# Order of a turn: two projection pieces directly behind the scores, then the transposes of both heads in one run

## The chip, the core and the metric

The kernel runs on one core of a Trainium2 chip. The core has several engines that run side by side, each through its own queue, in order: TensorE (PE in the rows; its weight loads are PEld), VectorE (DVE), ScalarE (ACT), GpSimd (POOL) and SyncE (SP, which issues DMAs here). They wait for each other only at semaphores. The metric is the device time of one execution in microseconds (us).

## The reference

Two layers over an input x of 8 sequences x 512 tokens x 256 channels. What the change touches is the attention of the first layer, with 16 heads of 64:

```python
q = _rmsnorm(q, q_rms_w); k = _rmsnorm(k, k_rms_w)      # after the projections x @ Wq, x @ Wk, x @ Wv
gate = softplus(einsum('bthd,hd->bht', k, u_n) / sqrt(D))
bias = -dist * omega_eff * gate                         # -inf above the diagonal
attn = softmax(q k^T * scale + bias)
y = attn @ v;  x = x + y @ Wproj + expert part
```

Beside it stand a first-layer expert part (32 experts, routed ahead of the attention, whose feed-forward is spread over the attention) and a second layer (memory read and routed feed-forward), which follows as a stage of its own.

## The kernel before, in words

The program has three stages: routing, attention (`attend`), second layer. Attention is a loop over 64 turns `s`: a turn is one sequence and one pair of heads (8 pairs per sequence). Each engine has its own loop over the same turns with its steps written out by hand; that text is the order. Nothing schedules it otherwise.

A turn is software-pipelined. In turn `s` TensorE does, in this order before the change:

- `all_scores(s)` (L939): scores of both heads into PSUM banks, in four causal chunks of 512, 256, 384 and 128 columns. It needs q and k of turn `s`, in a high and a low part (`qT_hi`, `kT_hi` from ScalarE; `qT_lo`, `kT_lo` from VectorE).
- `turn_p0(s-1)` (L978): 10 transposes of the probabilities of head 0 of the turn before, into three banks (4, 3 and 3 transposes).
- `project(s+2, 0)` and `project(s+2, 1)` (L926): 6 matmuls each; the projection of q, k, v and gate input for the turn after next, one 128-token piece each.
- `turn_p1(s-1)` (L978): 10 transposes for head 1.
- in some turns `turn_hidden` (L1025), then `project(s+2, 2)`.
- `values(s-1)` (L1006): probabilities times v. It waits for all six copies of transposed probabilities (`probT`): four by ScalarE (L1201), two by VectorE (L1371, one per head, the bank with the fifth to seventh transpose).
- the expert's matmuls (L1017 or L1034), the transposes of q, k and the gate columns for turn `s+1` (`turn_q` L959, `turn_k` L964, `turn_aug` L970), and `project(s+2, 3)`.
- in every eighth turn the output projection (L1050).

VectorE in a turn: `lows` (L1348, row minimum of the scores, 8 instructions in four pairs), and between them `mean_square(s+1)` (L1297 and L1300, sums of squares of q and k); `take_raw` (L1293, projection piece 0 from PSUM); `copy_p(s-1, 0)` (L1371); `newton_step` (L1304 to L1308, the inverse root, which waits for ScalarE's estimate); `copy_p(s-1, 1)` (L1371); then `copy_hidden` in some turns (L1388), gate input (L1316, L1318), `norm` (L1326), `gate` (L1322), `divide` (L1355, L1361), the expert's bias or output (L1383 or L1393), `copy_y` (L1377), `low_q` (L1333), `low_k` (L1338) and the second half of `divide`.

ScalarE in a turn: `square` (L1156), `exps(s,3)` and `exps(s,1)` (L1192), `copy_p` of head 0 (L1201 twice), `rsqrt(s+1)` (L1160, L1163: the estimate from the sums of squares), `take_raw` (L1149, piece 1), `copy_p` of head 1 (L1201 twice), further exponentials, `gate` (L1168, L1170), `copy_y` (L1206), `copy_q` (L1175), `copy_k` (L1179), `copy_aug` (L1183). In every fourth turn (`s % 4 == 2`, called gelu turn below) it puts `gelu` (L1210, with two table loads) ahead of the copies, and the exponentials behind them.

GpSimd's `augment` (L1479 to L1491) makes the gate columns `ag` from `gate`'s result; `turn_aug` on TensorE waits for them.

So four kinds of turn alternate, told apart by `s % 4`: 0 and 1 begin an expert (L1017), 2 is the gelu turn, 2 and 3 end an expert (L1025, L1034).

Of the kernel before, what the change touches and what calls it, by code (L numbers as in the profile page):

```python
# [674 lines left out]
def attend(nc, t, out, g):  # L675
# [5 lines left out]
    NTURN = B * HP  # L681
# [11 lines left out]
    with ExitStack() as ctx:  # L693
# [86 lines left out]
        def begins_in(s):  # L780

            return 2 * (s // 4) + s % 4 if s < NTURN and s % 4 < 2 else None

        def ends_in(s):

            return 2 * (s // 4) + s % 4 - 2 if s < NTURN and s % 4 >= 2 else None
# [44 lines left out]
        with nc.Block() as block:  # L831
# [80 lines left out]
            def _(eng):  # L912
# [70 lines left out]
                def turn_p0(s):  # L983
                    eng.wait_ge(p_done.sem, p_done.at(s, 1))
                    for i in range(3):
                        if s + 1 < NTURN:
                            eng.wait_ge(maxed.sem, maxed.at(s + 1, i + 1))
                        turn_p(s, 0, i)

                def turn_p1(s):  # L990
                    eng.wait_ge(p_done.sem, p_done.at(s, 2))
                    for i in range(3):
                        if s + 1 < NTURN:
                            eng.wait_ge(maxed.sem, maxed.at(s + 1, (4, 7, 8)[i]))
                        turn_p(s, 1, i)
# [103 lines left out]
                for s in range(NTURN + 1):  # L1099
                    if s < NTURN:  # L1100
                        all_scores(s)
                    else:
                        eng.wait_ge(y_done.sem, y_done.at(s - 2))
                        eng.wait_ge(eo_done.sem, eo_done.at(E - 1))
                    if s > 0:
                        turn_p0(s - 1)
                    if s + 2 < NTURN:
                        eng.wait_ge(o_done.sem, o_done.at((s - 1) // HP - 1))
                        project(s + 2, 0)
                    prepare(s, 0)  # L1110
                    if s + 2 < NTURN:
                        project(s + 2, 1)
                    prepare(s, 1)
                    if s > 0:
                        turn_p1(s - 1)
                    if ends_in(s) is not None:
                        turn_hidden(ends_in(s), s)
                    if s + 2 < NTURN:
                        project(s + 2, 2)
                    prepare(s, 2)  # L1120
                    if s > 0:
                        values(s - 1)
                    if begins_in(s) is not None:
                        hidden(begins_in(s), s)
                    if ends_in(s) is not None:
                        expert_output(ends_in(s), s)
                    if s + 1 < NTURN:
                        if s == 0:
                            eng.wait_ge(maxed.sem, maxed.at(0, 8))
                        turn_q(s + 1)  # L1130
                        turn_k(s + 1)
                        turn_aug(s + 1)
                    if s + 2 < NTURN:
                        project(s + 2, 3)
                    prepare(s, 3)
                    if 0 < s < NTURN and s % HP == 0:
                        for n in range(NT):
                            output(s // HP - 1, n)
# [3 lines left out]
            def _(eng):  # L1142
# [15 lines left out]
                def rsqrt(j):  # L1158
                    eng.wait_ge(ssd.sem, ssd.at(j))
                    eng.activation(lnv[:, :], ss[:, :], ACT.Ln).then_inc(r0_done.sem, 1)  # L1160
                    eng.wait_ge(newton.sem, newton.at(j - 1))
                    eng.wait_ge(r0_done.sem, r0_done.at(j, 1))
                    eng.activation(r0[:, :], lnv[:, :], ACT.Exp, scale=-0.5).then_inc(r0_done.sem, 1)  # L1163
# [31 lines left out]
                def copy_p(s, h, i):  # L1195
                    pe_p, done = (pe_p0, pe_p1)[h], (pt0_A, pt1_A)[h]
                    if h == 0 and i == 0:
                        eng.wait_ge(pe_y.sem, pe_y.at(s - 1))
                    eng.wait_ge(pe_p.sem, pe_p.at(s, i + 1))
                    x, y = segT[i]  # L1200
                    eng.activation(probT[h][:, x:y], bP[h][i][:, 0:y - x], ACT.Copy).then_inc(done.sem, 1)  # L1201
# [37 lines left out]
                for s in range(NTURN + 1):  # L1239
                    if s + 1 < NTURN:  # L1240
                        square(s + 1)
                    if s % 4 == 2:
                        gelu(s // 4)
                    elif s < NTURN:
                        exps(s, 3)
                        exps(s, 1)
                    if s > 0:
                        copy_p(s - 1, 0, 0)
                        copy_p(s - 1, 0, 2)
                    prepare(s, 0)  # L1250
                    if s + 1 < NTURN:
                        rsqrt(s + 1)
                    if s + 2 < NTURN:
                        take_raw(s + 2, 1)
                    prepare(s, 1)
                    if s > 0:
                        copy_p(s - 1, 1, 0)
                        copy_p(s - 1, 1, 2)
                    if s % 4 == 2:
                        exps(s, 3)  # L1260
                        gate(s + 1)
                        exps(s, 1)
                    if s < NTURN:
                        exps(s, 2)
                    if s + 1 < NTURN and s % 4 != 2:
                        gate(s + 1)
                    if s + 2 < NTURN:
                        take_raw(s + 2, 2)
                    prepare(s, 2)
                    if s < NTURN:  # L1270
                        exps(s, 0)
                    if s > 0:
                        copy_y(s - 1)
                    if s in (1, 2):
                        part = slice((s - 1) * HP // 2, s * HP // 2)
                        eng.wait_ge(wp_load.sem, wp_load.at(0))
                        eng.activation(wp_hi[:, part, :], proj_in[:, part, :], ACT.Copy).then_inc(wp_hi_done.sem, 1)
                    if s + 1 < NTURN:
                        copy_q(s + 1)
                        copy_k(s + 1)  # L1280
                        copy_aug(s + 1)
                    if s + 2 < NTURN:
                        take_raw(s + 2, 3)
                    prepare(s, 3)
# [3 lines left out]
            def _(eng):  # L1288
# [139 lines left out]
                for s in range(NTURN + 1):  # L1428
                    if s < NTURN:
                        lows(s, 3)  # L1430
                        lows(s, 1)
                    if s + 1 < NTURN:
                        mean_square(s + 1)
                    if s < NTURN:
                        lows(s, 2)
                        lows(s, 0)
                    if s + 2 < NTURN:
                        take_raw(s + 2)
                    prepare(s, 0)
                    if s > 0:  # L1440
                        copy_p(s - 1, 0)
                    prepare(s, 1)
                    if s + 1 < NTURN:
                        newton_step(s + 1)
                    if s > 0:
                        copy_p(s - 1, 1)
                    if ends_in(s) is not None:
                        copy_hidden(ends_in(s))
                    if s + 1 < NTURN:
                        gate_input(s + 1)  # L1450
                        norm(s + 1)
                        gate(s + 1)
                    if s < NTURN:
                        divide(s, 0)
                    if begins_in(s) is not None:
                        add_bias(begins_in(s))
                    prepare(s, 2)
                    if ends_in(s) is not None:
                        copy_expert_output(ends_in(s))
                    if s > 0:  # L1460
                        copy_y(s - 1)
                    if s + 1 < NTURN:
                        low_q(s + 1)
                        low_k(s + 1)
                    if s < NTURN:
                        divide(s, 1)
                    prepare(s, 3)
                    if 0 < s < NTURN and s % HP == 0:
                        for n in range(NT):
                            output(s // HP - 1, n)  # L1470
# [500 lines left out]
```

## Time and profile before

| what | value |
|---|---|
| executions, median of 3 | 1359.23 us (1357.82 to 1359.45) |
| profiled execution, span from the first to the last instruction | 1353.4 us |
| profiled execution's own time | not listed apart; the median is 5.8 us over the span |
| PE busy, share of the span | 97% |
| DVE busy | 81% |
| ACT busy | 70% |
| POOL busy | 14% |
| attention stage in the span | about 87 to 1085 us |

A matmul's row reads longer than the step from one to the next, since matmuls overlap in the array; the start times tell the pace. In a row, "xN" merges N like instructions, and "[0.23 <-PE at L926]" is idle time of the engine before the row and what ended it.

### The profile page before, as it was taken

How to read it: one execution, taken by the hardware profiler on the slowest of the kernel's cores; microseconds unless marked ns; L12 is line 12 of the kernel's file. 1: busy time of each engine (PE TensorE's matmuls, PEld its weight loads, DVE VectorE, ACT ScalarE, POOL GpSimd, SP SyncE). 2: the span in 40 equal slices, each digit the busy share in tenths (PEclk: the TensorE clock that was granted, in tenths of full speed). 3: DMA queues.
4: the chain of work that ended last, by engine and by line, in shares of the span. 5: the costliest groups of instructions: out<-in, count | busy, mean ns of one | idle time of the engine just before them, and what ended most of it. 6: DMA issues, size and time to landing. Idle time of an engine off the chain costs nothing. (4 is left out here: it accounts for less than half of the span.)

```text
span 1353.4 us, 32125 instructions
## 1 busy us (share of the span) xinstructions
PE 1309.2 (97%) x11499; PEld 1103.9 (82%) x11499; DVE 1090.3 (81%) x3337; ACT 947.7 (70%) x2376; POOL 190.3 (14%) x564
## 2 busy tenths in 40 slices
PE   5899999999999999999999999999999799999999
PEld 3688888887978888797888878888888588888888
DVE  6869996999699789969996998799699867777663
ACT  6759885888588678858885887688598724444333
POOL 4512111111011111101111111111111100000000
PEclk8889999999999999999999999999999999999999
DMA  6452231332323222322322233233232322111100
GB/s 216 171 173 88 73 132 59 110 116 74 102 74 131 80 89 87 104 88 88 119 93 92 84 102 109 67 108 103 77 99 72 108 82 62 55 56 55 55 17 32
DMA packets 90831, 125.17 MB, mean 92 GB/s; under 512 B 8761, under 2 KB 77105, under 8 KB 90673
## 3 DMA queue, kind: packets, MB, share of 16 engines
q1 hardware_dynamic: 90352, 123.11, 28.2%
q8 instruction: 93, 1.52, 0.5%
q14 instruction: 66, 0.53, 0.1%
q10 hardware_dynamic: 320, 0.00, 0.0%
HBM read 103.69 MB, written 19.40 MB: 91 GB/s over the span
## 5 line engine op out<-in xcount | busy, mean ns | idle before, releaser
L1192 ACT ACTIVATE prob<-prob,low 128x512 f32<-128x512 f32 (+3 forms) x512 | 280.8, 551 | 115.7 <-DVE low L1348 115.7
L1348 DVE CUSTOM_DVE_ANT_0 prob<-at,mask 128x512 f32<-128x512 f32 (+3 forms) x512 | 219.6, 485 | 10.3 <-PE at L939 10.3
L926 PE MATMUL at<-w_hi,c_lo 128*128 128x386 f32 x512 | 190.1, 371 | 1.5 <-DVE area_raw L1293 1.5
L926 PE MATMUL at<-w_hi,c_hi 128*128 128x386 f32 x512 | 174.3, 340 | 0.0
L926 PE MATMUL at<-w_lo,c_hi 128*128 128x386 f32 x512 | 174.0, 340 | 0.0
L1361 DVE TENSOR_SCALAR prob<-prob,rec 128x512 f32<-128x512 f32 (+3 forms) x512 | 169.3, 394 | 4.5
L978 PE MATMUL at<-ident,prob 128*128 128x128 f32 x1280 | 164.3, 275 | 3.2 <-DVE low L1348 1.8
L1006 PE MATMUL at<-probT,v 128*32 128x512 f32 (+3 forms) x2048 | 152.6, 438 | 3.8 <-DVE probT L1371 2.6
L978 PEld LDWEIGHTS at<-ident,prob 128*128 128x128 f32 x1280 | 142.4, 140 | 10.6 <-DVE yT_lo L1377 1.6
L1006 PEld LDWEIGHTS at<-probT,v 128*32 128x32 f32 x2048 | 67.3, 110 | 89.8 <-issue 80.7
L1201 ACT ACTIVATE probT<-at 128x512 f32<-128x512 f32 (+1 forms) x256 | 130.3, 536 | 4.4 <-PE at L978 1.5
L1479 POOL TENSOR_TENSOR slope<-gl,omega 128x8 f32<-128x8 f32 x64 | 12.8, 200 | 842.8 <-DVE gl L1322 821.9
L1149 ACT ACTIVATE area_raw<-at 128x386 f32<-128x386 f32 x192 | 93.4, 486 | 21.6 <-PE at L926 19.5
L926 PEld LDWEIGHTS at<-w_hi,c_lo 128*128 128x128 f32 x512 | 97.3, 190 | 2.2 <-DVE area_raw L1293 1.8
L926 PEld LDWEIGHTS at<-w_lo,c_hi 128*128 128x128 f32 x512 | 97.6, 191 | 0.1
L926 PEld LDWEIGHTS at<-w_hi,c_hi 128*128 128x128 f32 x512 | 96.8, 189 | 0.0
L1192 ACT ACTIVATION_READ_ACCUMULATOR prob<-prob,low 128x1 f32 x512 | 96.7, 189 | 0.0
L939 PE MATMUL at<-kT_hi,qT_hi 64*128 64x512 f32 (+3 forms) x512 | 86.6, 331 | 6.6 <-ACT kT_hi L1179 6.6
L939 PE MATMUL at<-kT_lo,qT_hi 64*128 64x512 f32 (+3 forms) x512 | 85.1, 326 | 1.5
L939 PE MATMUL at<-kT_hi,qT_lo 64*128 64x512 f32 (+3 forms) x512 | 84.7, 324 | 0.0
L939 PE MATMUL at<-kaug,qaug 64*128 64x512 f32 (+3 forms) x512 | 83.6, 319 | 0.0
L1297 DVE TENSOR_REDUCE ssq<-area_sq 128x16 f32<-128x1024 f32 x64 | 77.7, 1214 | 1.6 <-ACT area_sq L1156 1.6
(254 smaller groups left out, 3195.9 us busy)
## 6 DMA issues: line engine op xcount, KB each, us to landing
area_w<-in_L_ffn_w SPq DMA_DIRECT2D x65, 1024.0 KB, 5.5
bias<-in_L_ffn_w SPq DMA_DIRECT2D x160, 32.0 KB, 4.4
x_in<-in_L_attn_x SPq DMA_DIRECT2D x8, 512.0 KB, 5.5
xr<-in_L_attn_x SPq DMA_DIRECT2D x8, 512.0 KB, 4.6
eo_d<-hidT SPq DMA_DIRECT2D x32, 128.0 KB, 1.8
x_d<-xr SPq DMA_DIRECT2D x8, 512.0 KB, 2.9
area_raw<-x_d SPq DMA_DIRECT2D x8, 512.0 KB, 3.9
out<-area_raw SPq DMA_DIRECT2D x7, 512.0 KB, 3.1
```

What stands on the lines that cost most here:

```text
L926: m = eng.matmul(bQ[n % 2][:, 0:W], a[:, (j // HP) % 2, k, n * P:(n + 1) * P], w[:, k, j % HP, :], start=start, stop=(k == KC - 1 and a is ...
L939: m = eng.matmul(bC[i][:, at:at + (c + 1) * P], q[rows, c * P:(c + 1) * P], k[rows, 0:(c + 1) * P], start=ready is k_hi_done, stop=q is qaug)
L978: m = eng.transpose(bP[h][i][:, at:at + P], prob[s % 2][h][:, off[c] + kc * P:off[c] + (kc + 1) * P], ident[:, :])
L1006: m = eng.matmul(bY[rows, kc * P:T], v[:, s % 2, kc, rows], probT[j * E // D][:, offT[kc]:offT[kc + 1]], start=(kc == 0), stop=(kc == NT - 1))
L1149: eng.activation(raw[:, j % 2, n, :], bQ[n % 2][:, 0:W], ACT.Copy).then_inc(raw_A.sem, 1)
L1192: eng.activation(sl, sl, ACT.Exp, scale=-1.0, bias=low[:, i:i + 1], accum_out=den[:, i:i + 1]).then_inc(exp_done.sem, 1)
L1201: eng.activation(probT[h][:, x:y], bP[h][i][:, 0:y - x], ACT.Copy).then_inc(done.sem, 1)
L1297: eng.tensor_reduce(ss[:, :], sq[:, :, :].rearrange("p n (i d) -> p (n i) d", d=D), AX.X, ALU.add).then_inc(ssd.sem, 1)
L1348: eng.tensor_tensor_reduce(out=prob[s % 2][h][:, off[c]:off[c + 1]], in0=bC[i][:, at:at + (c + 1) * P], in1=mask[:, (NT - 1 - c) * P:T], s ...
L1361: p = eng.tensor_scalar(sl, sl, rec[:, k:k + 1], None, ALU.mult)
L1479: eng.tensor_tensor(slope32[:, :, :], gl[:, :, :], omega[:, hp * 2:hp * 2 + 2].unsqueeze(1).to_broadcast([P, NT, 2]), ALU.mult).then_inc(a ...
```

## The change

It changes only the order of steps in three of the engines' loops; no instruction is added or removed.

- TensorE: `turn_p0(s-1)` moves from directly behind the scores to behind `project(s+2, 1)`, directly ahead of `turn_p1(s-1)`.
- VectorE: `mean_square(s+1)` moves from between the `lows` to behind `copy_p(s-1, 0)`; `copy_p(s-1, 1)` comes ahead of `newton_step(s+1)`; `prepare(s, 1)` (used in the last turns only) comes ahead of both copies.
- ScalarE: all four `copy_p` stand together behind `take_raw(s+2, 1)`, and `rsqrt(s+1)` behind them.

```diff
@@ TensorE
-                    if s > 0:
-                        turn_p0(s - 1)
                     if s + 2 < NTURN:
                         eng.wait_ge(o_done.sem, o_done.at((s - 1) // HP - 1))
                         project(s + 2, 0)
...
                     prepare(s, 1)
                     if s > 0:
+                        turn_p0(s - 1)
                         turn_p1(s - 1)
@@ ScalarE
-                    if s > 0:
-                        copy_p(s - 1, 0, 0)
-                        copy_p(s - 1, 0, 2)
                     prepare(s, 0)
-                    if s + 1 < NTURN:
-                        rsqrt(s + 1)
                     if s + 2 < NTURN:
                         take_raw(s + 2, 1)
                     prepare(s, 1)
                     if s > 0:
+                        copy_p(s - 1, 0, 0)
+                        copy_p(s - 1, 0, 2)
                         copy_p(s - 1, 1, 0)
                         copy_p(s - 1, 1, 2)
+                    if s + 1 < NTURN:
+                        rsqrt(s + 1)
@@ VectorE
                         lows(s, 3)
                         lows(s, 1)
-                    if s + 1 < NTURN:
-                        mean_square(s + 1)
-                    if s < NTURN:
                         lows(s, 2)
                         lows(s, 0)
                     if s + 2 < NTURN:
                         take_raw(s + 2)
                     prepare(s, 0)
+                    prepare(s, 1)
                     if s > 0:
                         copy_p(s - 1, 0)
-                    prepare(s, 1)
+                    if s + 1 < NTURN:
+                        mean_square(s + 1)
+                    if s > 0:
+                        copy_p(s - 1, 1)
                     if s + 1 < NTURN:
                         newton_step(s + 1)
-                    if s > 0:
-                        copy_p(s - 1, 1)
```

VectorE's queue in a turn that ends an expert, before, from the last pair of `lows` on (the four rows of the 384- and 128-column `lows` have `mean_square` ahead of them):

```order
L1297 TENSOR_REDUCE ssq<-area_sq 128x16
L1300 TENSOR_SCALAR ssq<-ssq 128x16
L1348 ISA prob,low<-at,mask 128x384
...
L1293 COPY area_raw<-at 128x386
L1371 COPY probT<-at 128x384
L1304 SCALAR_TENSOR_TENSOR nw<-r 128x16
L1306 TENSOR_TENSOR nw<-nw,ssq 128x16
L1308 SCALAR_TENSOR_TENSOR rs<-nw,r 128x16
L1371 COPY probT<-at 128x384
L1388 COPY hidT<-at 128x256
```

And now (line numbers are two lower):

```order
L1291 COPY area_raw<-at 128x386
L1369 COPY probT<-at 128x384
L1295 TENSOR_REDUCE ssq<-area_sq 128x16
L1298 TENSOR_SCALAR ssq<-ssq 128x16
L1369 COPY probT<-at 128x384
L1302 SCALAR_TENSOR_TENSOR nw<-r 128x16
L1304 TENSOR_TENSOR nw<-nw,ssq 128x16
L1306 SCALAR_TENSOR_TENSOR rs<-nw,r 128x16
L1386 COPY hidT<-at 128x256
```

The sums of squares have moved from ahead of the last `lows` to between the two copies of `probT`, and the inverse root behind both.

ScalarE's queue in a gelu-free turn, from the exponentials to the next ones, before:

```order
L1192 ACTIVATE prob,dens<-prob,low 128x256 x2
L1201 ACTIVATE probT<-at 128x512
L1201 ACTIVATE probT<-at 128x384
L1160 ACTIVATE lnv<-ssq 128x16
L1163 ACTIVATE r<-lnv 128x16
L1149 ACTIVATE area_raw<-at 128x386
L1201 ACTIVATE probT<-at 128x512
L1201 ACTIVATE probT<-at 128x384
L1192 ACTIVATE prob,dens<-prob,low 128x384 x2
```

And now:

```order
L1191 ACTIVATE prob,dens<-prob,low 128x256 x2
L1148 ACTIVATE area_raw<-at 128x386
L1200 ACTIVATE probT<-at 128x512
L1200 ACTIVATE probT<-at 128x384
L1200 ACTIVATE probT<-at 128x512
L1200 ACTIVATE probT<-at 128x384
L1159 ACTIVATE lnv<-ssq 128x16
L1162 ACTIVATE r<-lnv 128x16
L1191 ACTIVATE prob,dens<-prob,low 128x384 x2
```

The logarithm and exponential of the sums of squares (`lnv`, `r`) now stand directly ahead of the next exponentials and behind all four copies.

TensorE's queue behind the scores shows one `L978 MATMUL at<-ident,prob 128x128 x20` behind the twelve L926 matmuls, where a run of ten stood ahead of them and a run of ten behind.

## Rows read from the trace of the kernel before

**Rows 1.** Table by stretch, turns 0, 2, 3 of four: PE, PEld, DVE, ACT, POOL, PEclk, DMA.
```profile
519.75:533.79 14.04, 14.04 (x137) 11.68 (x137) 12.98 (x43) 11.66 (x32) 2.24 (x8) 1.00 0.31 96
...
547.77:562.26 14.49, 14.18 (x139) 11.61 (x139) 13.07 (x43) 14.17 (x35) 2.10 (x7) 1.00 0.40 145
562.26:576.86 14.60, 14.50 (x138) 11.59 (x138) 13.85 (x45) 11.88 (x33) 2.24 (x8) 1.00 0.27 85
```

**Rows 2.** Timeline (start us, length us, ...) of TensorE, turn with `s % 4 == 0`.
```profile
522.27 0.27 PE L939 MATMUL at<-kaug,qaug 64*128 64x128 f32 x2
522.48 1.31 PE L978 MATMUL at<-ident,prob 128*128 128x128 f32 x10
...
525.62 0.34 PE L926 MATMUL at<-w_hi,c_hi 128*128 128x386 f32 x1
525.79 1.25 PE L978 MATMUL at<-ident,prob 128*128 128x128 f32 x10
526.80 0.42 PE L926 MATMUL at<-w_hi,c_lo 128*128 128x386 f32 x1
...
527.76 0.33 PE L926 MATMUL at<-w_hi,c_hi 128*128 128x386 f32 x1
528.09 2.36 PE L1006 MATMUL at<-probT,v 128*32 128x512 f32 x32
```

**Rows 3.** Timeline of TensorE, first turn, which has no transposes of probabilities.
```profile
89.57 0.44 PE L926 MATMUL at<-w_hi,c_lo 128*128 128x386 f32 x1
...
91.62 0.33 PE L926 MATMUL at<-w_hi,c_hi 128*128 128x386 f32 x1
```

**Rows 4.** Timeline of VectorE, the turn of rows 2.
```profile
523.13 1.22 DVE L1297 TENSOR_REDUCE ssq<-area_sq 128x16 f32<-128x1024 f32 x1
...
524.47 0.55 DVE L1348 CUSTOM_DVE_ANT_0 prob<-at,mask 128x384 f32<-128x384 f32 x1
...
526.32 0.55 DVE L1371 COPY probT<-at 128x384 f32<-128x384 f32 x1
526.78 0.16 DVE L1304 SCALAR_TENSOR_TENSOR nw<-r 128x16 f32<-128x16 f32 x1
...
527.28 0.55 DVE L1371 COPY probT<-at 128x384 f32<-128x384 f32 x1
...
531.42 0.42 DVE L1383 TENSOR_TENSOR hid<-at,bias 128x256 f32<-128x256 f32 x1 [0.58 <-issue]
...
532.71 0.75 DVE L1333 SCALAR_TENSOR_TENSOR qT_lo<-at,q_scale,qT_hi 128x512 fp32r<-128x512 f32 x1 [0.27 <-ACT qT_hi L1175]
```

**Rows 5.** Timeline of ScalarE, gelu turn (`s % 4 == 2`).
```profile
553.59 0.22 ACT L1160 ACTIVATE lnv<-ssq 128x16 f32<-128x16 f32 x1
...
555.41 0.71 ACT L1192 ACTIVATE prob<-prob,low 128x512 f32<-128x512 f32 x1
```

**Rows 6.** Timeline of TensorE: first transposes of gelu turn and next, scores between.
```profile
550.46 1.31 PE L978 MATMUL at<-ident,prob 128*128 128x128 f32 x10
...
562.26 0.50 PE L939 MATMUL at<-kT_hi,qT_hi 64*128 64x512 f32 x2 [0.31 <-ACT kT_hi L1179]
...
565.43 1.31 PE L978 MATMUL at<-ident,prob 128*128 128x128 f32 x10
```

**Rows 7.** Timelines of VectorE, GpSimd and weight loads, turn with `s % 4 == 3`.
```profile
570.37 0.55 DVE L1371 COPY probT<-at 128x384 f32<-128x384 f32 x1
...
572.58 0.16 DVE L1322 SCALAR_TENSOR_TENSOR gl<-gl,gp 128x8 f32<-128x8 f32 x1
...
574.40 0.21 POOL L1491 TENSOR_TENSOR ag<-shift,ag 128x8 fp32r<-128x8 f32 x1
...
575.17 0.44 PEld L970 LDWEIGHTS at<-ident,ag 128*68 128x68 f32 x4
```

**Rows 8.** Table by stretch, last turns of the attention (columns as in rows 1).
```profile
1069.00:1076.00 7.00, 4.46 (x34) 3.62 (x34) 5.64 (x21) 6.02 (x17) 0.00 (x0) 1.00 0.52 166
1076.00:1080.00 4.00, 3.61 (x32) 1.39 (x36) 2.56 (x8) 1.60 (x7) 0.00 (x0) 0.57 0.00 0
```

## The prediction

> **What bounds the kernel now.** I read the table by stretch first [rows 1]. A turn takes 14.0 us when `s % 4` is 0 or 1 (one of the two stands there), 14.5 us in the gelu turn and 14.6 us in the turn behind it; 64 turns make up some 1,000 us of the 1353.4 us span. TensorE shows busy for the whole of the first kind (14.04 of 14.04), at the full clock, so that kind looks bound by TensorE. VectorE is busy for 12.98 of 14.04 us, and for 13.85 of 14.60 in the last kind; ScalarE for 14.17 of 14.49 us in the gelu turn. Three engines are close to the length of a turn, so a new wait on VectorE or ScalarE has little room to be made good.
>
> Then the timelines show who is late. In the ordinary turn TensorE's last matmul of `project(s+2,2)` starts at 527.76, and `values` at 528.09 [rows 2]. The step from one such matmul to the next is 0.17 us (525.62 to 525.79), so `values` comes 0.16 us behind that. VectorE's second copy of `probT` starts at 527.28, takes 0.55 and ends at 527.83 [rows 4], 0.26 us ahead of `values`. I take it that this copy is what `values` waits for, and that 0.26 us is the way from its end to the matmul. So TensorE is full up to this point only because VectorE's copy is just in time. That is what I look at most.
>
> In the gelu turn the scores of the next turn wait for ScalarE's `kT_hi` with 0.31 us of idle time [rows 6]: there ScalarE sets the end, without a pause from the gelu on (14.17 us busy).
>
> **The change, part by part.** No instruction is added, so every cost is a wait or a switch.
>
> *TensorE alone.* Before: from the first transpose at 522.48 to the first matmul of `project(s+2,2)` at 526.80 are 4.32 us [rows 2]. After: I take the same gap behind the scores as now (0.21 us, 522.27 to 522.48) [rows 2]; the first turn has the two projection pieces there already, and its twelve matmuls take 89.57 to 91.62 plus 0.17, that is 2.22 us [rows 3]; two runs of ten transposes take 1.01 us each (525.79 to 526.80). Sum 4.24, a gain of 0.08 us a turn: one switch between transposes and matmuls less. Over 61 full turns that is 5 us, if nothing else is late.
>
> *VectorE's two copies, in each turn.* The copy of head 0 needs the seventh transpose of its head. That used to be done long before VectorE came. Now the transposes start at 522.48 + 2.22 = 524.70; the seventh starts six steps of 0.101 later, 525.31, takes the 0.275 us that the last of ten shows (1.25 less nine steps, rounded down) and ends at 525.58. I add 0.06 us for the signal and get 525.64 for the copy, where it was 526.32. VectorE is free 1.34 us earlier than before (`mean_square` left the place ahead: 523.13 to 524.47), at 524.98, and so idles for 0.66 us. Behind the copy (0.46 us to the next start, 526.32 to 526.78) comes `mean_square`, 1.34 us, and only then the copy of head 1: 525.64 + 0.46 + 1.34 = 527.44, against 527.28 [rows 4]. So `values` goes from 528.09 to 528.25: 0.16 us later, where TensorE alone would be 0.08 + 0.08 earlier. The inverse root (0.50 us, 526.78 to 527.28) has left the place ahead of the copy, but the idle time of 0.66 us is more than that.
>
> Everything on TensorE behind `values` is in order and shifts by the same 0.16 us, and the scores of the next turn with it. For 31 turns of the kinds 0 and 1: 31 x 0.16 = 5.0 us. In the kind 3 the first transposes are at 565.43 [rows 6]; by the same working the first copy starts at 565.43 + 2.22 + 0.88 + 0.06 = 568.59 and the second at 570.39, where it was 570.37 [rows 7], so nothing is lost or won at `values`. The bounds for this term: 0 when the signal comes at once and the copies run 0.1 us closer, 0.3 us a turn when each of two signals costs 0.1 us more.
>
> *The inverse root behind both copies.* The sums of squares are done about 1.42 us after `mean_square` starts (1.34 and the tail of its second instruction). ScalarE begins its logarithm 0.09 us later, and that and the exponential, 0.22 us each with a step between [rows 5], are done 0.57 us later, when `newton_step` may start; ScalarE's next instruction, whose start overlaps a little, follows 0.47 us behind the logarithm's start. In the ordinary turn: 526.10 + 1.42 + 0.09 + 0.57 = 528.18, plus 0.50 us for itself: gate input starts at 528.68, where it was 527.74. `norm`, `gate` and `divide` are 0.94 us later. What hides it: VectorE idles 0.58 us before `hid` and 0.27 us before `qT_lo` [rows 4], together 0.85, and these shift by 0.16 with TensorE: 1.01 against 0.94. Costs nothing, but the cover is used up.
>
> *GpSimd's gate columns.* In the kind 3, `gate` on VectorE starts at 572.58, the last of `ag` ends at 574.61 and TensorE's weights for `turn_aug` load at 575.17 [rows 7]: 0.56 us of slack. `gate` is later by 0.79 us (newton done at 568.59 + 0.46 + 1.42 + 0.09 + 0.57 + 0.50 = 571.63, where the queue was free at 570.37 + 0.47 = 570.84, one copy behind its start). So `ag` is done at 575.40, plus 0.08 for the signal: `turn_aug` is 0.3 us late, TensorE with it. 15 x 0.3 = 4.5 us. Bounds: 0 to 0.6 us a turn (GpSimd's spans are rough). In the kinds 0 and 1 the slack is as long as the delay, in the gelu turn the wait lies under ScalarE's.
>
> *ScalarE in the gelu turn.* This is the largest term. Transposes start at 550.46 + 2.22 = 552.68 [rows 6], VectorE's first copy at 552.68 + 0.88 + 0.06 = 553.62, `mean_square` at 554.08, its result at 555.50, logarithm 555.59, and the exponentials of the scores at 555.59 + 0.47 = 556.06, where they were at 555.41 [rows 5]: 0.64 us later. Before, `rsqrt` found its input ready; now it is behind four copies which wait for transposes, and then waits for the sums itself. From there ScalarE has no pause up to `copy_k`, on which the next scores wait. So all 0.64 us are on the path: 15 x 0.64 = 9.6 us. Bounds: 0.4 (TensorE's run and VectorE's copy 0.1 us earlier each) and 0.85. In the other kinds the same delay ends in ScalarE's idle time before `qT_hi`.
>
> *Last three turns.* They have few or no projections; `prepare` takes their place. VectorE and TensorE wait for each other for 1 us and more there, and I cost the edits at nothing, within 1 us either way.
>
> Sum: 5.0 + 4.5 + 9.6 = 19.1 us. Against the profiled execution: 1353.4 to 1372.5 us of span, 5.8 us around it, 1378.3 us. The median of the runs is 5.8 us over the profiled span, so I add 19.1 to 1359.2: 1378 us. The low bounds of the terms give 0 + 0 + 6 = 6 us (1365), the high ones 9.3 + 9 + 12.8 = 31 us (1390).
>
> **A rule against it: the clock.** TensorE had the full clock in all three turns of rows 1. In the last turns it had 1.00 from 1069 to 1076 us, while it was busy for 4.46 of 7.00 us, and 0.57 from 1076 to 1080 us [rows 8], a stretch at the lower of its two levels, 1.2 GHz against 2.4, behind transposes with waits between. Twenty transposes in one run make 2.0 us of such work. The Trainium skill, "TensorE: Matmul & The Clock Gate", Part 4: PE-mode transpose, says that transposes don't count as busy for the clock in the way matmuls do; by that rule a longer run would invite a fall. In rows 1 ten at a time, and twelve of another kind, do not.
>
> **The rivals.**
> *A. Faster.* VectorE's first copy is not held. All three costs hang on its start at 525.64. If it starts when its queue is free, at 524.98, the second copy is 0.5 us earlier than now, the sums come early enough for ScalarE and GpSimd, and `values` follows at TensorE's own pace: 0.16 us a turn in 31 turns and 0.08 in 30, 7 us, that is 1352. It decides below a start of about 525.2, where the gelu term is down to 0.2 us a turn. Against it: the seventh transpose behind twelve matmuls can't be done by then at the paces of rows 2 and 3. For it: TensorE shows as busy without a gap, so its rows may hide slack.
> *B. No difference.* The gain of TensorE and a delay of 0.2 us in gelu turns cancel: 1359, within 0.2%. For it: all other idle time is left. Against it: ScalarE's chain in the gelu turn has none.
> *C. The clock falls in each turn.* At half speed for some 3.4 us the 2.36 us of `values` would stretch by about 1.5 us (half of 3.4 us' work is left, with the waits taken off); over 61 turns some 90 us, 1450. Rows 8 show such a fall only with TensorE idle for a third of the time before it.
> *D. Only the gelu term is real*, and `values` and `ag` are in time: +6 to +10 us, inside my range.
>
> **How the numbers follow.** Forecast with its three terms 0.77, D 0.10, B 0.04, A 0.06, C 0.03. A measurement of this kernel tells 0.2% (2.7 us) from no change. Faster holds A: 0.06, and 0.01 for what I have not seen; same B with a part of D: 0.05; the rest, 0.88, is slower. The time is the forecast's, 1378. The range, 1364 to 1390, takes in the bounds of the terms and D; A, B and C are left out.
>
> **What would show it.** The page's row of `values` on TensorE (L1006) and of the copy of `probT` (L1369 then) with waits between them: VectorE idle about 0.6 us ahead of the first copy in each turn, ended by L978; `values` ending a wait for the copy. TensorE's twelve projection matmuls 0.21 us behind the scores. In the gelu turn, ScalarE's exponentials 0.6 us later against the scores' start, and the turn 15.1 us instead of 14.5. `turn_aug` idle 0.3 us in the turn behind it, ended by GpSimd. An ordinary turn of 14.2 us. The prediction is wrong if the ordinary turn is at or under 14.0 us (the first copy was not late), or if the gelu turn keeps its 14.5 us.

## The result, and the profile after

The changed kernel is slower. The first comparison gave 1374.46 us (median of 4, 1374.04 to 1377.49) against 1358.53 us for the kernel before, a ratio of 1.0157 with a 95% interval of 1.0122 to 1.0192. A second one, with more executions of both side by side, gave 1382.51 us against 1355.73 us, a ratio of 1.0213 (1.0182 to 1.0244). The forecast was 1378 us, within 1364 to 1390. The span of the profiled execution grew from 1353.4 to 1375.8 us.

The medians of one kernel move by some us from comparison to comparison. The stage ahead of the attention is the place: in the traces below, attention begins between 81.2 and 89.0 us, with one and the same code ahead of it, while the stretch behind it takes some 263 us in all twelve. So I compare ratios, and beside them the length of the attention stage alone (from the first scores to the last matmul group of `values`; before, that is from 86.9 to 1090.4 us), which is free of that: 1003.5 us before, 1026.9 us in the changed kernel, 1027.1 us in the second trace of it. The change costs 23.4 us there, a little more than the 19.1 us of the forecast.

The table by stretch of the changed kernel, one row for each kind of turn, `s % 4` of 0 to 3 (us, then busy us of PE, PEld, DVE, ACT and POOL, the granted clock, DMA share and GB/s), answers to [rows 1]:

```profile
529.63:543.86 14.23, 13.98 (x137) 11.65 (x136) 13.02 (x43) 11.96 (x32) 2.24 (x8) 1.00 0.32 94
543.86:558.07 14.21, 13.98 (x138) 11.62 (x138) 13.15 (x43) 11.96 (x32) 2.11 (x7) 1.00 0.26 87
558.07:573.23 15.16, 14.34 (x139) 11.86 (x139) 12.90 (x43) 14.53 (x35) 2.09 (x7) 1.00 0.40 142
573.23:588.11 14.88, 14.78 (x138) 11.82 (x138) 14.00 (x45) 12.22 (x33) 2.25 (x8) 1.00 0.24 80
```

The ordinary turn (`s % 4` of 0 or 1) grew by 0.19 us (the second one by 0.23, from 13.98), the gelu turn by 0.67, the turn behind it by 0.28. These are single turns; over all 31 ordinary ones the growth is 0.27 us a turn. The granted clock is 1.00 in all four rows. TensorE is no longer busy for the whole of an ordinary turn.

TensorE's timeline in the first of these turns answers to [rows 2]; the twelve projection matmuls stand ahead of the run of twenty now:

```profile
534.56 2.34 PE L978 MATMUL at<-ident,prob 128*128 128x128 f32 x20
536.66 0.42 PE L926 MATMUL at<-w_hi,c_lo 128*128 128x386 f32 x1
...
538.20 2.36 PE L1006 MATMUL at<-probT,v 128*32 128x512 f32 x32 [0.25 <-DVE probT L1369]
```

Counted from the scores' start (529.63), `values` begins at 8.57 us, where it was 8.34 (528.09 less 519.75), and now its row itself says what it waited for: VectorE's copy of `probT`. VectorE's timeline of the same turn answers to [rows 4]:

```profile
534.28 0.56 DVE L1291 COPY area_raw<-at 128x386 f32<-128x386 f32 x1
535.59 0.56 DVE L1369 COPY probT<-at 128x384 f32<-128x384 f32 x1 [0.75 <-PE at L978]
536.06 1.21 DVE L1295 TENSOR_REDUCE ssq<-area_sq 128x16 f32<-128x1024 f32 x1
...
537.39 0.55 DVE L1369 COPY probT<-at 128x384 f32<-128x384 f32 x1
538.07 0.18 DVE L1302 SCALAR_TENSOR_TENSOR nw<-r 128x16 f32<-128x16 f32 x1
...
541.73 0.41 DVE L1381 TENSOR_TENSOR hid<-at,bias 128x256 f32<-128x256 f32 x1
...
542.83 0.75 DVE L1331 SCALAR_TENSOR_TENSOR qT_lo<-at,q_scale,qT_hi 128x512 fp32r<-128x512 f32 x1
```

The first copy is held by the transposes for 0.75 us, the sums of squares queue behind it, the second copy behind them. The idle times before `hid` (0.58 us) and `qT_lo` (0.27 us) of [rows 4] are gone: no more cover. ScalarE in the gelu turn answers to [rows 5]:

```profile
563.69 2.18 ACT L1200 ACTIVATE probT<-at 128x512 f32<-128x512 f32 x4
565.95 0.22 ACT L1159 ACTIVATE lnv<-ssq 128x16 f32<-128x16 f32 x1
...
566.38 0.71 ACT L1191 ACTIVATE prob<-prob,low 128x512 f32<-128x512 f32 x1
```

The exponentials start 8.31 us behind the scores' start (558.07), where it was 7.64 (555.41 less 547.77). TensorE's next scores pay for it, in a row that answers to [rows 6]:

```profile
573.23 0.50 PE L939 MATMUL at<-kT_hi,qT_hi 64*128 64x512 f32 x2 [0.81 <-ACT kT_hi L1178]
```

The idle time rose from 0.31 to 0.81 us. In the turn behind, GpSimd's last `ag` row and the weights of `turn_aug` answer to [rows 7]:

```profile
586.24 0.21 POOL L1488 TENSOR_TENSOR ag<-shift,ag 128x8 fp32r<-128x8 f32 x1
...
586.51 0.36 PEld L970 LDWEIGHTS at<-ident,ag 128*68 128x68 f32 x4 [0.22 <-POOL ag L1488]
```

### The profile page after: what moved, and what is told of

The parts are those of the page before. It is cut to its first block and busy times, and to the rows that moved or that the text cites. A ratio compares the mean times of both kernels' runs of the same rounds, so it can differ in the third digit from the quotient of the medians.

```text
span 1375.8 us, 32125 instructions
## 1 busy us (share of the span) xinstructions
PE 1314.2 (96%) x11499; PEld 1107.9 (81%) x11499; DVE 1095.4 (80%) x3337; ACT 967.2 (70%) x2376; POOL 190.0 (14%) x564
## 5 line engine op out<-in xcount | busy, mean ns | idle before, releaser
L1346 DVE CUSTOM_DVE_ANT_0 prob<-at,mask 128x512 f32<-128x512 f32 (+3 forms) x512 | 215.3, 485 | 10.6 <-PE at L939 10.6
L926 PE MATMUL at<-w_hi,c_lo 128*128 128x386 f32 x512 | 191.3, 374 | 0.2 <-DVE area_raw L1291 0.2
L926 PE MATMUL at<-w_hi,c_hi 128*128 128x386 f32 x512 | 174.0, 340 | 0.0
L926 PE MATMUL at<-w_lo,c_hi 128*128 128x386 f32 x512 | 173.6, 339 | 0.0
L1359 DVE TENSOR_SCALAR prob<-prob,rec 128x512 f32<-128x512 f32 (+3 forms) x512 | 165.1, 386 | 4.5
L1006 PE MATMUL at<-probT,v 128*32 128x512 f32 (+3 forms) x2048 | 154.1, 441 | 10.5 <-DVE probT L1369 10.2
L978 PE MATMUL at<-ident,prob 128*128 128x128 f32 x1280 | 150.6, 273 | 1.9 <-DVE prob L1359 1.4
L1006 PEld LDWEIGHTS at<-probT,v 128*32 128x32 f32 x2048 | 72.3, 110 | 95.2 <-issue 87.4
L978 PEld LDWEIGHTS at<-ident,prob 128*128 128x128 f32 x1280 | 143.4, 140 | 5.0 <-DVE yT_lo L1375 1.6
L1200 ACT ACTIVATE probT<-at 128x512 f32<-128x512 f32 (+1 forms) x256 | 135.0, 545 | 5.5 <-PE at L978 1.8
L1476 POOL TENSOR_TENSOR slope<-gl,omega 128x8 f32<-128x8 f32 x64 | 12.8, 200 | 866.5 <-DVE gl L1320 846.3
L1369 DVE COPY probT<-at 128x384 f32<-128x384 f32 x128 | 70.7, 553 | 40.3 <-PE at L978 40.1
L926 PEld LDWEIGHTS at<-w_hi,c_lo 128*128 128x128 f32 x512 | 97.0, 189 | 5.1 <-DVE area_raw L1291 0.5
L926 PEld LDWEIGHTS at<-w_lo,c_hi 128*128 128x128 f32 x512 | 97.4, 190 | 0.1
L926 PEld LDWEIGHTS at<-w_hi,c_hi 128*128 128x128 f32 x512 | 96.6, 189 | 0.0
```

The source lines that it names most:

```text
L926: m = eng.matmul(bQ[n % 2][:, 0:W], a[:, (j // HP) % 2, k, n * P:(n + 1) * P], w[:, k, j % HP, :], start=start, stop=(k == KC - 1 and a is ...
L978: m = eng.transpose(bP[h][i][:, at:at + P], prob[s % 2][h][:, off[c] + kc * P:off[c] + (kc + 1) * P], ident[:, :])
L1006: m = eng.matmul(bY[rows, kc * P:T], v[:, s % 2, kc, rows], probT[j * E // D][:, offT[kc]:offT[kc + 1]], start=(kc == 0), stop=(kc == NT - 1))
L1346: eng.tensor_tensor_reduce(out=prob[s % 2][h][:, off[c]:off[c + 1]], in0=bC[i][:, at:at + (c + 1) * P], in1=mask[:, (NT - 1 - c) * P:T], s ...
L1359: p = eng.tensor_scalar(sl, sl, rec[:, k:k + 1], None, ALU.mult)
L1369: eng.tensor_copy(probT[h][:, x:y], bP[h][1][:, 0:y - x]).then_inc(done.sem, 1)
```

## The experiments

All ratios are against the kernel before, timed in the same set of runs. The last four columns are lengths of one turn of each kind in the traces, in us, `s % 4` of 0 to 3. Expected totals take the kernel before at 1359 us; since its median was 1355.4 to 1355.7 in these sets, I judge them by their distance from it.

| kernel | attention stage, us | ratio, 95% interval | 0 | 1 | gelu | behind it |
|---|---|---|---|---|---|---|
| before | 1003.5 | 1 | 14.04 | 13.98 | 14.49 | 14.60 |
| changed | 1026.9 | 1.0157 (1.0122 to 1.0192) | 14.23 | 14.21 | 15.16 | 14.88 |
| changed, again | 1027.1 | 1.0213 (1.0182 to 1.0244) | 14.31 | 14.23 | 15.15 | 14.88 |
| TensorE's edit only | 1022.0 | 1.0171 (1.0130 to 1.0213) | 14.25 | 14.22 | 15.17 | 14.74 |
| VectorE's edit only | 1085.1 | 1.0618 (1.0569 to 1.0668) | 15.20 | 15.17 | 16.07 | 15.62 |
| ScalarE's edit only | 1109.8 | 1.0782 (1.0719 to 1.0845) | 15.87 | 15.82 | 15.97 | 16.33 |
| changed, sums early | 1011.5 | 1.0089 (1.0054 to 1.0124) | 14.06 | 14.00 | 14.98 | 14.71 |
| changed, sums last | 1087.5 | 1.0631 (1.0582 to 1.0681) | 15.22 | 15.21 | 16.19 | 15.91 |
| changed, one piece | 1016.3 | 1.0082 (1.0049 to 1.0114) | 13.99 | 14.00 | 15.00 | 14.69 |
| sums and root early | 1001.5 | 0.9968 (0.9941 to 0.9994) | 13.95 | 13.95 | 14.54 | 14.66 |
| and fourth copy by VectorE | 995.0 | 0.9942 (0.9916 to 0.9969) | 13.94 | 13.94 | 14.16 | 14.60 |
| and q, k copies first | 987.7 | 0.9872 (0.9837 to 0.9908) | 13.95 | 13.90 | 14.16 | 14.24 |

**Sums early.** VectorE as in the kernel before up to the copies, the two copies together:

```diff
                         lows(s, 1)
+                    if s + 1 < NTURN:
+                        mean_square(s + 1)
...
                         copy_p(s - 1, 0)
-                    if s + 1 < NTURN:
-                        mean_square(s + 1)
-                    if s > 0:
                         copy_p(s - 1, 1)
```

> The changed kernel with VectorE's mean_square back between the lows, and its two copies of probT directly one after the other; TensorE and ScalarE as changed. Theory (VectorE's first copy is late behind twelve matmuls, and the sums of squares queued behind it are what costs): the copies no longer wait, values comes at about 8.2 us from the scores' start (8.34 before, about 8.6 changed), ordinary turn 13.9 us, the turn behind the gelu turn about 14.6, gelu turn 14.9 (ScalarE's rsqrt still stands behind four copies, 0.4 us late). Total 1360 us, within 1356 to 1364. Rival 1 (TensorE's new order, a run of twenty transposes behind the projection pieces, costs by itself): stays at 1370 or more. Rival 2 (the place of ScalarE's rsqrt is the whole cost): gelu turn stays 15.1, total above 1368.

Two thirds of the cost are gone (15.4 of 23.4 us in the stage), so TensorE's order with twenty transposes in a row does not cost that by itself. `values` now starts 8.26 to 8.28 us behind the scores, earlier than before. But the stage is 8.0 us over the kernel before, where the expectation had 1 (the median, 1364.82 us, is over the stated 1364 too): a miss. VectorE's row shows part of the reason.

```profile
547.06 1.06 DVE L1369 COPY probT<-at 128x384 f32<-128x384 f32 x2
548.83 0.17 DVE L1302 SCALAR_TENSOR_TENSOR nw<-r 128x16 f32<-128x16 f32 x1 [0.70 <-ACT r L1162]
```

VectorE waits 0.70 us for ScalarE's root in each turn (41.2 us in all), since that stands behind four copies. The gelu turn, 14.98, recovered only 0.18 of 0.67 us: the rest is ScalarE's exponentials, late because the root and they stand behind the four copies, whether the sums are early or not.

**Sums and root early.** The same, and on ScalarE:

```diff
                         take_raw(s + 2, 1)
                     prepare(s, 1)
+                    if s + 1 < NTURN:
+                        rsqrt(s + 1)
                     if s > 0:
                         copy_p(s - 1, 0, 0)
...
-                    if s + 1 < NTURN:
-                        rsqrt(s + 1)
```

> As the one before, and ScalarE's rsqrt moved to between take_raw of piece 1 and the four copies, where it fills the time until the transposes are done. Theory: ordinary turn 13.9 us, gelu turn 14.5 to 14.6 (exponentials within 0.1 us of their old place), turn behind it 14.5. Total 1354 us, within 1350 to 1358, faster than the kernel before by the saved switch and the wait of values. Rival (TensorE's order saves nothing or costs): at or above the kernel before, 1359.

As the theory had it: ordinary turns of 13.95 us, `values` at 8.26, the gelu turn within 0.05 us of before. This is TensorE's new order with no one late, and it is faster than the kernel before by 0.3% (the interval excludes 1, by little), 2.0 us in the stage, where about 5 were expected. The 31 ordinary turns give 1.7 of it.

**TensorE's edit only.** VectorE and ScalarE as before.

> Only TensorE's edit; VectorE's and ScalarE's order as in the kernel before. Theory: VectorE's own copies are not late, since the sums stand ahead of them: second copy at 7.5 us from the scores' start as before, ordinary turn 14.0 to 14.1. ScalarE's first copy in the gelu turn waits 0.4 to 0.5 us for the later transposes, gelu turn 14.9. Total 1365 us, within 1360 to 1369. Rival 1 (TensorE's order is the cost): 1374 like the changed kernel. Rival 2 (a later first transpose costs nothing at all): 1355 to 1359.

A miss: 1.0171, and 18.5 us in the stage, three times the expected 6. VectorE's copies are not held, as I had said, but ScalarE's are, and `values` waits for the last of them. ScalarE's timeline, then TensorE's:

```profile
528.53 1.09 ACT L1200 ACTIVATE probT<-at 128x512 f32<-128x512 f32 x2 [0.87 <-PE at L978]
529.52 0.21 ACT L1159 ACTIVATE lnv<-ssq 128x16 f32<-128x16 f32 x1
529.82 0.21 ACT L1162 ACTIVATE r<-lnv 128x16 f32<-128x16 f32 x1
529.98 0.49 ACT L1148 ACTIVATE area_raw<-at 128x386 f32<-128x386 f32 x1
530.37 0.98 ACT L1200 ACTIVATE probT<-at 128x512 f32<-128x512 f32 x2
```

```profile
531.49 1.06 PE L1006 MATMUL at<-probT,v 128*32 128x512 f32 x8 [0.25 <-ACT probT L1200]
```

ScalarE idles 0.87 us for the first transposes, and root, piece 1 and two more copies follow one behind the other; the last copy ends at 531.35. The expectation had counted a wait of ScalarE in the gelu turn only (0.4 to 0.5 us; it is 0.68 there) and none that matters in the ordinary turns, which came to 14.25 and 14.22. So late transposes have a second price at ScalarE, apart from the one at VectorE.

**VectorE's edit only, ScalarE's edit only.** Each takes the kernel before and makes the edit of one engine only (in words):

```diff
 VectorE's only: mean_square behind copy_p(s - 1, 0), newton_step behind copy_p(s - 1, 1)
 ScalarE's only: take_raw(s + 2, 1), four copy_p, rsqrt(s + 1), in this order
```

In VectorE's, `prepare(s, 1)` stays between the two copies, behind `mean_square`; it plays a part in the last turns only.

> Only VectorE's edit (mean_square behind its first copy, newton_step behind the second); TensorE's and ScalarE's order as in the kernel before. Theory: the sums are done at 7.5 us from the scores' start; ScalarE's rsqrt stands ahead of take_raw and of the copies of head 1 and holds them, so values comes at 9.6 us (8.34 before), ordinary turn 15.3 us, gelu turn 16.3 us. Total 85 us over the kernel before, within 65 to 105. Rival (the place of the sums does not matter, TensorE's order is all of the cost): within 5 us of the kernel before.

> Only ScalarE's edit (all four copies behind take_raw of piece 1, rsqrt behind them); TensorE and VectorE as in the kernel before. Theory: VectorE's newton_step stands ahead of its copy of head 1 and now waits for rsqrt behind four copies, so that copy comes at 9.4 us and values at 10.2 us; every turn 1.6 to 1.9 us longer, 105 us over the kernel before, within 80 to 130. So the three edits would be cheaper together (23 us in the traces) than two of them alone. Rival (queues have room for it): within 15 us of the kernel before.

Both came out as worked: 81.6 and 106.3 us more in the stage (85 and 105 expected), `values` at 9.49 and 10.16 us from the scores' start (9.6 and 10.2). One of the four executions of the second took 3260.59 us; nothing here explains it, and the ratio leaves it out. The waits of the first and of the second kernel (engine and line, what it waited for, us in total, times, longest) name the links:

```profile
ACT lnv L1160 <- DVE ssq L1300: 117.0, 64, 2.8
...
PE at L1006 <- ACT probT L1201: 66.9, 61, 1.3
```

```profile
DVE nw L1303 <- ACT r L1163: 105.7, 63, 2.0
...
PE at L1006 <- DVE probT L1370: 92.4, 63, 1.9
```

The three edits alone cost 18.5, 81.6 and 106.3 us, together 23.4. So they can't be added up.

**Sums last.** The changed kernel with the sums behind both copies:

```diff
                         copy_p(s - 1, 0)
-                    if s + 1 < NTURN:
-                        mean_square(s + 1)
-                    if s > 0:
                         copy_p(s - 1, 1)
                     if s + 1 < NTURN:
+                        mean_square(s + 1)
                         newton_step(s + 1)
```

> The changed kernel with mean_square behind both copies of probT on VectorE (directly ahead of newton_step). It takes the wait of values for the second copy away and makes the sums about 1 us later. Theory (the sums, and by them the inverse root, exponentials and gate columns, are the larger part of the cost): values comes at 8.2 us, but turn_aug waits for GpSimd by over 1 us in every turn; ordinary turn about 15.2 us, gelu turn 16.2, total 1444 us, within 1420 to 1460. Rival (the wait of values for the second copy is the cost): 1360 to 1368, faster than the changed kernel.

`values` no longer waits (8.25 us), and yet the kernel is slower by 6.3%: sums of squares that are later by the second copy cost far more than the wait of `values` that they replace. That holds for sums as late as these; it doesn't rank the parts in the changed kernel. The stage is 84 us over the one before; turn lengths of 15.2 and 16.19 are the expected ones. GpSimd's gate columns are what ends the wait:

```profile
PEld at L970 <- POOL ag L1486: 68.1, 64, 1.1
```

**One piece.** A dose: only piece 0 ahead of the first ten transposes.

In words:

```diff
 TensorE:  scores, project(s + 2, 0), turn_p0, project(s + 2, 1), turn_p1
 ScalarE:  copies of head 0, take_raw(s + 2, 1), copies of head 1, rsqrt
```

> The changed kernel with only one projection piece between the scores and the transposes of head 0 (piece 1 stands between the two runs of ten, ScalarE's copies of head 0 ahead of take_raw again, rsqrt behind all copies); VectorE as changed. Theory (a dose: the first run starts at 3.9 us from the scores' start, 2.7 before and 4.9 changed): VectorE's first copy no longer waits, values at 8.3 us, ordinary turn 14.0; rsqrt behind the copies makes the gelu turn 15.0 and the one behind it 14.8. Total 10 us over the kernel before, within 4 to 15. Rival (VectorE's place for mean_square costs by itself, wherever the transposes stand): 20 us or more.

1.0082, 12.8 us in the stage, where 10 (4 to 15) were expected. Ordinary turns are back at 14.0; what is left is in the gelu turn and behind it, from `rsqrt` behind the copies, as in the kernel with sums early (14.98 and 14.71 there, 15.00 and 14.69 here).

**Fourth copy by VectorE; q and k copies first.** Both build on sums and root early, and act in gelu turns only:

```diff
 ScalarE, first kernel:
                         copy_p(s - 1, 1, 0)
-                        copy_p(s - 1, 1, 2)
+                        if s % 4 != 2:
+                            copy_p(s - 1, 1, 2)
                     if s % 4 == 2:
                         exps(s, 3)
-                        gate(s + 1)
                         exps(s, 1)
+                        gate(s + 1)
 VectorE, first kernel: copies segment 2 of head 1 behind its copy_p(s - 1, 1) if s % 4 == 2
 ScalarE, second kernel: exps(s, 0) behind copy_aug(s + 1) if s % 4 == 2, otherwise in its place
```

> The kernel with sums and root early (two pieces behind the scores, twenty transposes in one run), and in gelu turns VectorE makes ScalarE's fourth copy of probT, and ScalarE's gate stands behind the exponentials of chunk 1. It tests that ScalarE's chain sets the end of the gelu turn. Theory: 0.4 us less on ScalarE's chain, gelu turn 14.2 us instead of 14.54, the turn behind it 14.3 instead of 14.64; 8 us less than the kernel with sums and root early, 10 us less than the kernel before (4 to 12). Rival (the gelu turn is set by VectorE's kT_lo or by TensorE): no difference, or slower by the added 0.4 us of VectorE.

> As the kernel in which VectorE makes a fourth copy in gelu turns, and in gelu turns ScalarE's last exponentials (chunk 0) stand behind copy_y, copy_q, copy_k and copy_aug. Theory: the turn behind the gelu turn is still 14.60 us, 0.3 longer than its work, since its third scores matmul waits for VectorE's kT_lo, which waits for ScalarE's copy_y and copy_q; with these 0.45 us earlier the head of the scores is not stretched: turn behind the gelu turn 14.2 to 14.3, gelu turn unchanged at 14.16; 5 us less than that kernel, 14 us less than the kernel before (9 to 17). Rival (the stretch is VectorE's own work): no difference.

The first took the gelu turn from 14.54 to 14.16, as expected, and left the turn behind at 14.60, where I had expected 14.3: the stage is 6.5 us under the kernel with sums and root early (8 expected) and 8.5 under the kernel before (10, within 4 to 12). It moves two steps at once, the fourth copy and `gate`; what each is worth alone was not run. TensorE's scores come as much earlier as ScalarE's copies do, so VectorE's `kT_lo` is late by as much as before: the third scores matmul starts 0.55 us behind the second.

```profile
552.94 0.68 DVE L1337 TENSOR_TENSOR kT_lo<-at,kT_hi 128x512 fp32r<-128x512 f32 x1
...
553.12 0.46 PE L939 MATMUL at<-kT_hi,qT_lo 64*128 64x512 f32 x2
553.67 0.50 PE L939 MATMUL at<-kT_lo,qT_hi 64*128 64x512 f32 x2
```

In the second kernel that step is 0.23 us, as in an ordinary turn:

```profile
550.35 0.39 PE L939 MATMUL at<-kT_hi,qT_lo 64*128 64x512 f32 x2
550.58 0.40 PE L939 MATMUL at<-kT_lo,qT_hi 64*128 64x512 f32 x2
```

The turn behind the gelu turn is 14.24 now, and the stage 15.8 us under the kernel before (14, within 9 to 17). The table by stretch of the second kernel, the four kinds of turn:

```profile
508.00:521.95 13.95, 13.95 (x138) 11.42 (x138) 13.09 (x43) 11.54 (x32) 2.25 (x8) 1.00 0.31 96
521.95:535.85 13.90, 13.90 (x137) 11.39 (x136) 13.04 (x43) 11.54 (x32) 2.11 (x7) 1.00 0.24 86
535.85:550.01 14.16, 14.16 (x139) 11.64 (x139) 13.77 (x45) 13.44 (x31) 2.11 (x7) 1.00 0.41 152
550.01:564.25 14.24, 14.24 (x139) 11.58 (x139) 13.34 (x44) 12.14 (x36) 2.25 (x8) 1.00 0.27 86
```

TensorE is busy for the whole of each kind of turn. The kernel is faster than the one before by 1.3% (0.9872, 0.9837 to 0.9908), median 1336.24 us.

**The changed kernel again.**

> The changed kernel itself once more, timed beside the kernel before in the same runs. The first comparison gave 1.0157 from 4 executions each, while the attention stage of the two profiled executions differs by 23.4 us, 1.7%. If the attention is the only place of the difference and the stage ahead of it scatters by itself by some us, the ratio of many runs is 1.016 to 1.019. Rival (the trace of the changed kernel caught an unusually long attention): 1.012 or less.

1.0213, above the range that I gave: a miss. The stage was the same to 0.2 us, so the rival is out. The agreement is partly chance: one turn of this trace, the fourth, took 16.30 us instead of about 14.9 at a granted clock of 0.90, and the end of the stage was 1.6 us shorter than in the first trace. The stage by itself is good to some 1.5 us. What makes the ratio higher than 1.7% no trace here shows; the stage ahead of the attention is the only other one seen to vary.

## Why the prediction was right, point by point

**VectorE's two copies: right, somewhat small.** I put the first copy at 5.89 us from the scores' start (525.64 less 519.75); it came at 5.96 and 5.93. The transposes start where I had them (4.93 us from the scores' start, 4.95 forecast); the copy follows 1.03 us behind instead of 0.94, partly because a step between transposes is 0.109 us and not 0.101 (see TensorE alone). From there the working held: 1.80 us to the second copy, 0.26 from its end to `values`, which came 0.23 us later instead of 0.16. Over all 31 turns the term is 8.5 us, where I had 5.0 and at most 9.3. In the turn behind the gelu turn `values` came 0.12 us later, where I had nothing.

**The cover for the inverse root: right.** The two idle times were used up (rows above), and the ordinary turn of these rows grew by no more (0.19 us) than `values` is late (0.23).

**GpSimd's gate columns: right.** 0.28 us in the turn behind the gelu turn (0.3 forecast), 4.2 us in all (4.5), with the wait shown. That the delay runs over the sums is shown by the kernel with sums last, where the same wait appears in every turn.

**ScalarE in the gelu turn: right in size (0.67 us against 0.64), half right in its cause.** I let the chain run over VectorE's late sums. With the sums early the gelu turn is still 14.98, 0.49 over the kernel before; only with `rsqrt` ahead of the copies too it is 14.54. Two paths arrive nearly together: the sums, and ScalarE's own four copies behind late transposes. ScalarE's rows of the kernel with sums early part the two:

```profile
560.22 2.18 ACT L1200 ACTIVATE probT<-at 128x512 f32<-128x512 f32 x4
562.29 0.21 ACT L1159 ACTIVATE lnv<-ssq 128x16 f32<-128x16 f32 x1
```

The logarithm starts 2.07 us behind the first copy there and 2.26 us in the changed kernel (563.69 to 565.95, above). So the sums are 0.19 us of the 0.67, and the root behind four copies of late transposes is 0.48. Taking away one leaves the other. The kernel with TensorE's edit only has a gelu turn of 15.17 by the second path alone.

**TensorE alone: wrong, by a small term.** I had counted a gain of 0.08 us a turn and put it down to a switch less between transposes and matmuls. The kernel with sums and root early, where no one is late, shows TensorE's own pace:

```profile
521.78 0.44 PE L926 MATMUL at<-w_hi,c_lo 128*128 128x386 f32 x1
...
524.03 2.35 PE L978 MATMUL at<-ident,prob 128*128 128x128 f32 x20
526.13 0.42 PE L926 MATMUL at<-w_hi,c_lo 128*128 128x386 f32 x1
```

From the first of these to `project(s+2,2)` are 4.35 us, against 4.32 before [rows 2]: nothing saved. The twelve matmuls take 2.25 us (2.22 forecast), and took that before as well, as the first of them shows, 523.54 to 525.79:

```profile
523.54 0.42 PE L926 MATMUL at<-w_hi,c_lo 128*128 128x386 f32 x1
```

The twenty transposes take 2.10 us (2.02 forecast). That is a misreading of [rows 2]. I divided the 1.01 us of a run of ten (525.79 to 526.80) by ten. The run's row is 1.25 us long and a single transpose 0.275 (the mean on the page), so nine steps make 0.975 us, 0.108 each, and the next matmul starts only 0.03 us behind the last transpose. A run of twenty is nineteen such steps (2.34 less 0.275 is 2.07, 0.109 each) and that short one. Two runs have the short step twice, one run has it once: 2 x 1.01 is 0.08 us too little. What its ordinary turns win (13.95 us against 14.04 and 13.98) is the wait of `values` for VectorE's second copy, 8.26 us from the scores' start instead of 8.34. I had named that wait and given it the right size, 0.08.

**The sum.** By the single turns shown, 15 x 0.19 + 16 x 0.23 + 15 x 0.67 + 15 x 0.28 = 20.8 us; the stage grew by 23.4. Over all turns of the two traces the sum closes: 8.5 us in the 31 ordinary turns, 10.1 in the 15 gelu turns that are followed by a full turn, 4.2 in the 15 behind them, and 0.7 at the ends of the stage (0.7 in the first turn, nothing in the last two together, as forecast). The single ordinary turns shown are among those that grew least. One turn with the output projection stands out, 25.93 us against 25.58 to 25.61 in the other six (25.37 before). The total of 19.1 was close because the gelu and gate terms were; only the copies' term was far off, and inside its bounds. That 1378 us lies between the two medians, 1374.46 and 1382.51, owes something to the scatter.

**The rivals.** C is out: in the changed kernel's first trace the granted clock is 1.00 in each of the 61 turns in which projections and twenty transposes stand in a row. In its second trace the clock falls once, to 0.50 from 128.4 to 131.8 us, behind an idle time of TensorE of 1.75 us that ended with `kT_hi`, not in a run of transposes; the kernel with one piece, with ten transposes at a time, shows two such falls. By the rule of the Trainium skill ("TensorE: Matmul & The Clock Gate", Part 4: PE-mode transpose) the longer run might have invited one in each turn; these traces don't show that. A and B are excluded by both comparisons; that the first copy's start decides, as A said, is true, but it needed ScalarE's order as well. D (only the gelu term) is excluded by the ordinary turns.

## What to carry to other kernels

A step that is moved later on a busy engine is late for every in-order queue that takes its result, and everything behind it in those queues is late too, wanted or not: work out each consumer, with the item that stands behind the wait. If a wait is put into a queue, fill the time ahead of it with work whose input is ready (here the root, and the sums ahead of the copies), rather than move that work behind it. Three edits to three queues are one edit: singly they cost 18.5, 81.6 and 106.3 us, together 23.4, and TensorE's with a better place for two of the others' steps gains 2.0. And read the pace of a merged row from its start times or its length less one member, not from the whole divided by the count.

## What the runs showed that I had not expected

The gain was in the gelu turn and the one behind it, not in the order under study: with one copy of 0.4 us given to VectorE, `gate` put behind exponentials, and ScalarE's last exponentials put behind its copies of q and k, two kinds of turn lost 0.38 and 0.42 us (14.54 to 14.16, 14.66 to 14.24). And the stage ahead of the attention, the same in all these kernels, ended between 81.2 and 89.0 us in the twelve traces. That scatter is a third of the change's effect. And a run of twenty transposes takes 2.10 us, no less than two runs of ten (1.06 and 1.01 us).
